# Scan input of a selective state-space layer moved from VectorE products to float32r TensorE products over rows laid out in DRAM

## The reference

```python
dt = soft_clamp(softplus(xc @ W_dt.T + b_dt), 0.001, 0.1, 0.5)
Bp, Cp = xc @ W_B.T, xc @ W_C.T
dA = exp(soft_clamp(dt[..., None] * A, -8.0, 8.0, 0.5))
dB = dt[..., None] * Bp[:, :, None, :]
def step(h, inp):                                  # h: 2 x 512 x 16
    h = h * dA_t + dB_t * x_t[:, :, None]
    nrm = sqrt(sum(h * h, axis=(1, 2)))
    fac = minimum(20.0 / (nrm + 1e-08), 1.0)
    h = where(t % 10 == 0, h * fac, h)
    y = einsum('bdn,bn->bd', h, C_t) + D_param * x_t
```

## Time and profile before

| | |
|---|---|
| median of 3 runs | 1652.79 us (1650.85 to 1653.66) |
| profiled execution, its own time | 1652.22 us |
| its span | 1650.4 us |
| PE, PE weight loads, DVE, ACT, POOL busy | 1382, 1056, 1388, 1268, 978 us |
| mean granted TensorE clock | 0.991 |

### The profile page before, as it was taken

The page is one execution under the profiler, slowest core; times in us unless marked ns, Lnnn a source line. Parts: engine busy times, 40 slices in busy tenths (PEclk is TensorE's granted clock), DMA queues, the critical chain, the costliest instruction groups (busy, mean ns, idle before and its releaser), DMA issues.

```text
span 1650.4 us, 24684 instructions
## 1 busy us (share of the span) xinstructions
PE 1382.1 (84%) x7160; PEld 1055.6 (64%) x7160; DVE 1387.6 (84%) x1684; ACT 1268.5 (77%) x3354; POOL 978.3 (59%) x1318
## 2 busy tenths in 40 slices
PE   6999999999577787778777777777777877799998
PEld 5555555553366666666666666666666666677776
DVE  7757655645599999999999999999999999987885
ACT  4454455558899999999999999999999996433333
POOL 1302222112388888988888888888888888800000
PEclk9999999999799999999999999999999999999999
DMA  7223356224244333433433342434243235565430
GB/s 244 77 78 97 111 148 165 76 92 143 73 122 112 84 93 91 105 80 102 108 86 93 92 105 75 109 85 105 77 113 83 79 89 160 154 205 160 147 115 26
DMA packets 202694, 179.88 MB, mean 109 GB/s; under 512 B 82816, under 2 KB 175040, under 8 KB 202560
## 3 DMA queue, kind: packets, MB, share of 16 engines
q1 hardware_dynamic: 201616, 176.99, 38.7%
q10 hardware_dynamic: 944, 1.31, 0.2%
HBM read 125.26 MB, written 53.57 MB: 108 GB/s over the span
## 4 chain that ended last, share of the span: by engine, by line
DVE 44%; PE 29%; issue 17%; ACT 6%; POOL 3%; DMA 1%; DVEq 0%; ACTq 0%; SPq 0%; POOLq 0%
DVE h L1042 35%; PE banks L326 7%; PE banks L318 5%; PE banks L293 4%; ACT tb L924 3%; PE banks L1185 3%; PE banks L1206 3%; DVE cv L585 3%; PE banks L1216 2%; DVE banks L1031 2%; PE banks L333 2%; POOL hc L826 1%; PE banks L867 1%; ACT sc_sq L934 1%; PE banks L281 1%
## 5 line engine op out<-in xcount | busy, mean ns | idle before, releaser
L1042 DVE TENSOR_TENSOR_SCAN h<-decay,banks 128x704 f32<-128x704 f32 x410 | 660.2, 1610 | 9.7 <-ACT banks L960 9.2
L867 PE MATMUL banks<-hc,w_ident 128*128 128x160 f32 (+1 forms) x3296 | 611.9, 309 | 18.2 <-POOL hc L826 17.7
L826 POOL TENSOR_TENSOR hc<-h,bc 128x640 f32<-128x640 f32 x410 | 590.8, 1441 | 0.0
L867 PEld LDWEIGHTS banks<-hc,w_ident 128*128 128x128 f32 x3296 | 485.5, 191 | 38.8 <-POOL hc L826 29.9
L924 ACT ACTIVATE tb<-dtc,a 128x320 f32<-128x320 f32 (+1 forms) x832 | 448.8, 556 | 4.8 <-DVE x L552 4.8
L1031 DVE TENSOR_TENSOR banks<-banks,bc 128x640 f32<-128x640 f32 x408 | 339.6, 833 | 44.4 <-issue 14.5
L850 PE MATMUL banks<-sc_ss,sc_ones 128*128 128x1 f32 x820 | 156.0, 259 | 215.3 <-ACT sc_sq L934 207.5
L850 PEld LDWEIGHTS banks<-sc_ss,sc_ones 128*128 128x128 f32 x820 | 123.2, 189 | 307.4 <-ACT sc_sq L934 303.3
L952 ACT ACTIVATE decay<-tb 128x640 f32<-128x640 f32 x410 | 298.1, 728 | 0.4
L818 POOL TENSOR_TENSOR rc<-qs,w_mhalf 128x1 f32<-128x1 f32 x410 | 226.8, 553 | 61.7 <-POOL qs L813 1.3
L236 POOL TENSOR_TENSOR ln_rz<-ln_vz,w_mhalf 128x4 f32<-128x4 f32 x8 | 13.9, 1734 | 280.8 <-DVE ln_vz L558 280.8
(11 more groups left out here) (109 smaller groups left out, 1621.0 us busy)
## 6 DMA issues: line engine op xcount, KB each, us to landing
bc<-scratch_blk SPq DMA_DIRECT2D x205, 320.0 KB, 3.5
uc<-scratch_u SPq DMA_DIRECT2D x35, 240.0 KB, 4.5
scratch_xc<-xc SPq DMA_DIRECT2D x8, 1024.0 KB, 4.8
scratch_sg<-sg SPq DMA_DIRECT2D x8, 1024.0 KB, 5.9
scratch_dt<-dt SPq DMA_DIRECT2D x8, 1024.0 KB, 6.2
scratch_u<-u SPq DMA_DIRECT2D x8, 1024.0 KB, 6.9
q_ys<-scratch_y SPq DMA_DIRECT2D x8, 1024.0 KB, 6.0
q_xc<-scratch_xc SPq DMA_DIRECT2D x8, 1024.0 KB, 8.8
```

What stands on the lines that cost most here:

```text
L826: pool.tensor_tensor(hc[:, pl % 2, :, j % 2 * S:(j % 2 + 1) * S] .rearrange("p (c b n) e -> p c b n e", c=KE, b=B)[:, :, b], state(m)[:, : ...
L867: mm = pe.matmul(psY[:, 0:KE * B * wide], w.ident[:], rhs, start=(n == 0), stop=(n == N - 1))
L1042: dve.tensor_tensor_scan(state(m).rearrange("p r e -> p (r e)"), decay[:, m % DRING], psI[m % B][:, 0:NCH * W], 0.0, ALU.mult, ALU.add).th ...
```

## The change

The products u*B leave DVE. u and B of 128 steps of one batch (a **piece**, 32 in all) are read back from DRAM, turned by PE so that steps lie on partitions (`turn_piece`), and split into a high float32r part (`high_piece` on ACT) and the remainder (`low_piece` on DVE). POOL multiplies B by a 0/1 mask that puts it at the place of its step within the block (`mask_piece`). Four DMAs write rows of 688 numbers to DRAM (`store_piece`), four rows for each step (high and low u by high and low B). For each unit `load_unit` brings 40 such rows into `ub`, of which the other 88 partitions stay zero, and `inputs(m + 2)` on PE makes the unit's 4 x 176 inputs by four float32r products. Pieces 0 and 1 are turned in the pre-stage behind `project_dt(4)` and `project_dt(5)`, pieces 2 to 31 at units 2, 14, 26, ..., 350.

`squares` moves from ACT to DVE, as a product of the last step with itself. `readout` takes four blocks at once: 16 products of 320 columns for 8 units. `repeat` and `move_u` go. In the pre-stage the tanh of dt is written in place, so that `softplus(i)` waits for dt of tile i - 1; the `masks` are built by DVE in tile 4; `bc` holds C alone, so its loads are half as large.

```diff
+            if i in (4, 5):
+                scan.load_piece(sp, i - 4)
+            if i in (5, 6):
+                scan.store_piece(sp, i - 5)
...
+            if i == 6:
+                scan.load_units(sp)
+                scan.load_piece(sp, 2)
...
+            if i in (5, 6):
+                scan.mask_piece(pool, i - 5)
...
+            if i in (4, 5):
+                scan.turn_piece(pe, i - 4, psD.rearrange("p k c -> p (k c)"))
...
-        scan.squares(act, 0)
-        scan.squares(act, 1)
...
+def piece_unit(k):
+
+    return 12 * (k - B) + 2
...
-    psU = banks[:, 2:4]
+    psT = banks[:, 2:4].rearrange("p k c -> p (k c)")
...
+    def load_unit(sp, m):
+        j, b = m // B, m % B
+        sp.wait_ge(ub_out, 64 * (B * (min((j + 1) * S, L - 1) // P) + b + 1))
+        if m >= URING:
+            sp.wait_ge(inp_ready, m - URING + 1)
+        sp.dma_start(ub[m % URING][0:SPLITS * S, :].bitcast(F32),
+                     dram["ub"][b, j * S + 1:(j + 1) * S + 1].rearrange("t v x -> (t v) x")
+                     ).then_inc(ub_in[m % URING], 16)
...
+    def turn_piece(pe, k, out):
+        pe.wait_ge(piece_in, 32 * (k + 1))
+        if k >= 1:
+            pe.wait_ge(ut_lo, k)
+        for c in range(KE):
+            pe.transpose(out[:, c * P:(c + 1) * P], piece[:, c, :], w.ident[:])
+        pe.transpose(out[:, E:E + 2 * N], piece_b[:], w.ident[0:2 * N, 0:2 * N]).then_inc(ut_done, 1)
+
+    def high_piece(act, k, src):
+        act.wait_ge(ut_done, k + 1)
+        if k >= 1:
+            act.wait_ge(ub_out, 64 * k)
+            act.wait_ge(spread_done, k)
+        act.activation(turned[:, 0, :], src[:, 0:E + N], ACT.Copy).then_inc(ut_hi, 1)
+
+    def low_piece(dve, k, src):
+        dve.wait_ge(ut_hi, k + 1)
+        dve.tensor_tensor(turned[:, 1, :], src[:, 0:E + N], turned[:, 0, :].bitcast(F32), ALU.subtract).then_inc(ut_lo, 1)
+
+    def mask_piece(pool, k):
+        pool.wait_ge(ut_lo, k + 1)
+        if k == 0:
+            pool.wait_ge(mask_steps, 2 + 2 * (S // 2))
+        if k >= 1:
+            pool.wait_ge(ub_out, 64 * k)
+        pool.tensor_tensor(
+            spread[:], turned[:, :, E:].bitcast(F32).unsqueeze(3).broadcast_to([P, 2, N, W]),
+            mask[:, k // B % (S // 2)].unsqueeze(1).unsqueeze(1).broadcast_to([P, 2, N, W]),
+            ALU.mult).then_inc(spread_done, 1)
+
+    def store_piece(sp, k):
+        t, b = k // B * P, k % B
+        rows = dram["ub"][b, t:t + P].rearrange("t (r h) x -> t r h x", h=2)
+        sp.wait_ge(ut_lo, k + 1)
+        for r in range(2):
+            sp.dma_start(rows[:, r, :, 0:E], turned[:, :, 0:E].bitcast(F32)).then_inc(ub_out, 16)
+        sp.wait_ge(spread_done, k + 1)
+        for half in range(2):
+            sp.dma_start(rows[:, :, half, E:], spread[:].bitcast(F32).rearrange("p r n e -> p r (n e)")
+                         ).then_inc(ub_out, 16)
+
...
+            if m - 1 in pieces:
+                mask_piece(pool, pieces[m - 1])
...
-        def move_u(g):
-            pe.wait_ge(u_in[g % 2], 16 * (g // 2 + 1))
-            if g >= 2:
-                pe.wait_ge(inp_ready, (g - 1) * HB * B)
-            pe.matmul(psU[:, g % 2, 0:KE * B * HALF], w.ident[:], uc[g % 2][:].rearrange("p a t -> p (a t)"),
-                      start=True, stop=True).then_inc(u_moved, 1)
+        def inputs(m):
+            pe.wait_ge(ub_in[m % URING], 16 * (m // URING + 1))
+            if m >= B:
+                pe.wait_ge(h_ready, m + 1)
+            for c in range(KE):
+                mm = pe.matmul(psI[m % B][:, c * N * W:(c + 1) * N * W], ub[m % URING][:, c * P:(c + 1) * P],
+                               ub[m % URING][:, E:], start=True, stop=True)
+            mm.then_inc(inp_ready, 1)
...
-        def repeat(p, m):
-
-
-            pe.wait_ge(q_copied, m + 1)
-            rhs = hc[:, p % 2].rearrange("p (c n) t -> p c n t", n=N)[:, :, 0]
-            pe.matmul(psQ[:, P:P + KE * B * 2 * S], w.ident[:], rhs, start=True, stop=True)
...
         for m in range(UNITS):
             if m + B < UNITS:
                 total(m + B)
-            if m % (HB * B) == 4 and m // (HB * B) + 1 < HALVES - 1:
-                move_u(m // (HB * B) + 1)
-            p, quarter = (m - 4) // 4, m % 4
+                inputs(m + B)
+            if m in pieces:
+                turn_piece(pe, pieces[m], psT)
...
+            p, part = m // (QB * B) - 1, m % (QB * B)
             if p >= 0:
-                readout(p, quarter * 4, quarter * 4 + 3)
-                if m < UNITS - 6:
-                    repeat(p, m + B)
-                readout(p, quarter * 4 + 3, quarter * 4 + 4)
-        for p in range((UNITS - 4) // 4, PAIRS):
-            readout(p, (UNITS % 4) * 4 if p == (UNITS - 4) // 4 else 0, N)
+                readout(p, part * each, (part + 1) * each)
...
-            if m + B < UNITS:
-                squares(act, m + B)
-            if m % 4 == 0 and m >= 8:
-                copy_y((m - 8) // 4)
+            if m % (QB * B) == 0 and m >= 2 * QB * B:
+                copy_y(m // (QB * B) - 2)
...
+            if m in pieces:
+                high_piece(act, pieces[m], psT)
...
-        def inputs(m):
-            j, b = m // B, m % B
-            g, o = j // HB, j % HB * S
-            u = psU[:, g % 2, 0:KE * B * HALF].rearrange("p (c b t) -> p b c t", b=B, t=HALF)
-            if g == HALVES - 1:
-                u = uc[g % 2][:].rearrange("p (c b) t -> p b c t", b=B)
-            if j % HB == 0 and b == 0:
-                if g < HALVES - 1:
-                    dve.wait_ge(u_moved, g + 1)
-                else:
-                    dve.wait_ge(u_in[g % 2], 16 * (g // 2 + 1))
-            if b == 0:
-                dve.wait_ge(bc_in[j % RING], 16 * (j // RING + 1))
+        def squares(m):
+            b = m % B
+            dve.wait_ge(h_ready, m + 1)
             if m >= B:
-                dve.wait_ge(h_ready, m + 1)
-            dve.tensor_tensor(
-                inp(m)[:, :, 1:].rearrange("p (c n) e -> p c n e", c=KE),
-                u[:, b, :, o:o + S].unsqueeze(2).broadcast_to([P, KE, N, S]),
-                bc[j % RING][:, 0, b].unsqueeze(1).broadcast_to([P, KE, N, S]),
-                ALU.mult).then_inc(inp_ready, 1)
+                dve.wait_ge(sum_ready, m - B + 1)
+            last = state(m - B)[:, :, S]
+            dve.scalar_tensor_tensor(out=sq[:, b, :], in0=last, scalar=1.0, in1=last, op0=ALU.mult, op1=ALU.mult,
+                                     accum_out=ss[:, b:b + 1]).then_inc(sq_ready, 1)
...
             scan(m)
             if m + B < UNITS:
-                inputs(m + B)
+                squares(m + B)
+            if m - 1 in pieces:
+                low_piece(dve, pieces[m - 1], psT)
```

231 lines of the change are left out of this document (143 added, 88 removed).

## The result

The changed kernel takes 1706.9 us (median of 4 runs, 1706.1 to 1707.6) against 1652.3 us before: 3.3% slower, ratio 1.033 with a 95% interval of 1.031 to 1.035. The profiled execution has a span (first to last instruction) of 1705.6 us, 55.2 more than before. The forecast was 1686, with a range of 1658 to 1745.

What follows compares the result with a forecast made beforehand. POOL's slot of 2.38 us was taken as the scan's bound; -18 + 29 + 9 + 11 - 1 + 4 = +34 on 1652.2 gave 1686 us, own range 1662 to 1712, 8 in 10 1658 to 1745.

Steps and rivals of the forecast that it cites:

- the bound on POOL: In the scan, POOL's slot from weigh to weigh has a floor of 2.38 us, whatever DVE does.
- a fall of the clock: Sign on PE's granted clock: if it falls, the forecast is wrong.
- First stage, +11: Pre-stage tiles 4 and 5: PE waits for the piece's load and transposes it, 2 x 5.5 us; bounds 2 and 14.
- -1 at the start of the scan: At the start of the scan ACT's two first squares fall away, 1 us less.
- Masks, +29: On POOL in the scan, 30 mask_piece products of 0.97 us with gap, hidden by nothing; bounds 6 and 43.
- the sign of 3.3 to 3.7: In the scan, weigh to weigh should take 3.3 to 3.7 us where a mask falls in.
- Late copies, +9: high_piece on ACT makes POOL's norm 0.3 us late at 30 pieces; from 0 to 18 us.
- Gains on DVE and ACT, -18: Scan excess above POOL's slot falls: 9.4 us in ordinary units, 2 at borders, 4 in first slots, 3 in last.
- the first rival: Squares on DVE blocked by weigh, from borders to the next mask 1742 us, for good about 1950; chance 0.16.
- I expect its granted clock to stay at 1.00: PE in the scan is as busy as before without repeat, 80%, so its clock should not fall.
- Tail, +4: After the last unit, 14 readout products of 320 columns remain instead of 12 of 160: 7.5 us against 3.27.
- the race that the prediction called close: After blocked squares, scan and squares need 1.57 to 1.65 us, the path to the next weigh 1.61.

Runs made afterwards that it cites:

- The early loads: Changed kernel with the loads of the first two pieces put ahead of the stores of tiles 4 and 5 in SyncE's queue: 1691.1 us.
- squares unblocked and no mask: Changed kernel with squares reading its operand once (a plain sum, no squaring) and the masks of 30 pieces left out: 1663.9 us.
- one-input squares: Changed kernel with squares as a plain sum of the last steps, reading one operand, the squaring left out: 1676.8 us.
- the small product: Changed kernel with one more unread product of 128 columns a unit on PE: 1702.2 us, ratio 1.0295.
- The clamp off POOL: Changed kernel with the clamp of the norm moved from POOL into ScalarE's copy of the sum: 1889.6 us.
- one wait that fixes the order: Changed kernel with the clamp moved from POOL to ScalarE and weigh(m) waiting for squares(m + 3): 1680.9 us.
- the later pieces: Changed kernel with clamp on ScalarE, weigh waiting for squares, first two pieces loaded early, each piece's low half and mask one unit later: 1632.0 us.

## Why the prediction was right, and where it was not

Right in sign, in the order of the three places of loss (scan, first stage, tail) and in the main number: the bound on POOL. The time of 1706.9 lies inside the range, but 55 us were lost where 34 were forecast, and the sum came as near as it did partly by luck, since two misses in the scan work against each other (below). By its own signs the forecast is also wrong in one place: it named a fall of the clock, and the clock fell. POOL's slot of 2.38 was forecast as 2.37 to 2.40 and measured as 2.38 to 2.40; DVE under 85% (77 to 79); squares of 0.27 where 0.3 was taken; PE's input products 0.13 us apart where 0.14 was taken (four in 0.53), so that neither PE nor DVE became the bound. An ordinary slot of 2.38 was 2.38 before as well, so the relief on DVE and ACT could only take from the excess above it.

Point by point against the sum:

- **First stage, +11 (and -1 at the start of the scan).** Measured +13.0 to the first `weigh`. The wait of tile 4 was 4.48 for 4.6, that of tile 5 3.70. What the term lacked is the clock behind the waits: in tile 4 the work that follows ran at half the clock and took another 2.3 us (7.0 instead of 4.7), in tile 5 1.0. The early loads took 9.2 off the 13.0. In the 3.9 that are left stand the transposes of the pieces, 0.85 us in each tile, and a last dt projection of 16.85 us where before it took 15.67.
- **Masks, +29.** The long slot at a piece is 3.15 to 3.2 us, below the sign of 3.3 to 3.7 that the forecast gave, and the slots at 28 pieces lost 27.5 us together. That is near the 29, but these slots hold the late copies too (38 for both, at 30 pieces), and the step is wrong all the same. Leaving the mask out changed 1.7 us. The step "POOL. This is where the change puts work that nothing hides" failed: something hid it, the wait for squares that `low_piece` had pushed behind `weigh`. The prediction had the mechanism as a rival, and even wrote that a mask "pushes it back"; it did not see that the piece itself sets it off, 26 times of 30.
- **Late copies, +9.** With squares unblocked and no mask, a piece still costs 0.31 us, 9 in all. The size was right, but for another reason than the one given, which is luck: by the timeline the delay came by way of `low_piece` waiting 0.98 us for `high_piece`, more than by the norm's copy.
- **Gains on DVE and ACT, -18.** Away from the pieces the scan did not gain but lost 9 us. The slots up to 2.58 us did give back some of their excess (2.6 us in 256 of them, before 5.2 in 269). The first 24 slots got 5.5 us longer and the borders 4.5, where squares are blocked. With one-input squares all slots away from the pieces have 13.2 us of excess, before 30.0: 16.8 less, so the term was sound, and nearly of the right size, where the block is absent. (The stretch has 12 chunk borders and not 11, which leaves 8.5 and not 9.4 for ordinary slots; and 11 x 6 x 0.8 is 53, not the 56 of the first rival.)
- **Clock, "I expect its granted clock to stay at 1.00".** It did not: 0.95 to 0.97. The reasoning compared PE's busy share (80% before and after) and took the share for what keeps the clock. In the changed kernel PE is 83% busy in the scan, and the clock falls behind idle stretches, of 1.92 us at 760.30 and of 4.48 us in tile 4. The kernel of before without `repeat` has a clock of 0.83 to 0.88 in the scan with no blocked squares at all, so waits for blocked squares are not the only cause. What it cost here is small, some 5 us in the scan by the small product, and the 2.3 and 1.0 us in tiles 4 and 5.
- **Tail, +4.** Measured 5.7; the readout itself 4.3.

The mis-sized term is the scan's: +20 forecast (-18 + 29 + 9), +36.5 measured. The gap of 16 is made of two misses. Away from the pieces the scan has +9 for some -18, and the pieces have 27.5 for 38. The first is the first rival in part: 20 blocked squares outside the pieces and the slow slots behind them. That rival was right on the cause, the 0.26 us by which the squares win, and on what happens when they lose; it was wrong in that the block would go on from unit to unit. Behind 42 of the 46 blocked squares the next ones are free. They win the next race, in most cases by only 0.02 to 0.06 us (761.81 against 761.83), the race that the prediction called close. The other four follow one another from 1464 us on, in five slots of 3.15 to 3.45 us. There a product of the post-stage stands on DVE between the squares and the next scan, and takes 0.68 us:

```profile
1464.12 0.71 DVE L1142 SCALAR_TENSOR_TENSOR sc_sq<-h 128x64 f32<-128x64 f32 x1
...
1464.77 0.68 DVE L1423 TENSOR_TENSOR q_ys<-q_ys,q_sg 128x512 f32<-128x512 f32 x1
...
1465.37 1.61 DVE L1150 TENSOR_TENSOR_SCAN h<-decay,banks 128x704 f32<-128x704 f32 x1
```

So the scan comes late, and the next squares lose again. The clamp off POOL shows how near the block was: 0.34 us less on the bound engine, and 398 of 410 squares are blocked.

Do the parts add up? With blocks and masks both gone the span is 12.6 us above that of before: 12.9 up to the first `weigh`, -6.3 in the scan and 6.0 behind it. So the scan of the change, without masks and blocks, is faster than before by 6.3 us, where the forecast without its masks has 9 (-18 + 9). The early loads, 15.8 by the medians, would bring that kernel to some 1648, but the two were never run together. How the 42.9 divides between block and mask has no answer, since they lie over each other.

## What to carry to other kernels

When two engines hand work round a loop, measure by how much one instruction wins against the one that can block it, before giving the bound engine less to do: here 0.34 us less on POOL cost 183 us, and the same edit with one wait that fixes the order ran in 1680.9, 26 less than without either. (It took the early loads and the later pieces to reach 1632.) A long slot with a suspicious instruction in it is not yet that instruction's fault; take the instruction out, and if the slot stays, look for what arrives late beside it. A piece of periodic work whose input is not there yet may cost less one unit later: here it took the slots at the pieces from 57.1 us of excess to 22.4.

## What the hardware showed that was not expected

- A DVE operation on 64 elements with two SBUF inputs took 0.70 to 1.53 us beside POOL's two-input product, and its own 0.27 us began 0.14 to 0.15 us ahead of that product's end in all 46 cases (759.00 + 1.24 - 0.27 against 758.67 + 1.44). With one SBUF input (265 ns) it was never held up in 410. POOL's power with one element a partition does not block it: at 1221.76 it starts, and the squares at 1222.13 take 0.28.
- It works the other way too: `weigh` took 1.52 to 1.58 us instead of 1.44 where the squares had started 0.02 to 0.06 us ahead of it (761.83).
- Leaving out a product nobody reads cost 25.7 us (1.5%) and took the granted clock of the scan, by windows of 100 us, from 1.00 to between 0.83 and 0.88, with no change in the ordinary slot.
- Float32r products of 176 columns followed each other by 0.13 us on average in the changed kernel, against 0.228 for 512 columns.
- With the clamp off POOL, ScalarE's activation with an accumulator took 0.25 us and 0.19 more for the read on two elements, against 0.16 for the plain copy of one in the changed kernel.
